# Next batch's layer norm and splits spread over several bodies of an attention kernel, its loops unrolled

## The reference, cut to what matters

```
a = layer_norm(ctx, gamma, beta)            # over the 1024 features
Q, K, V = x @ Wq.T, a @ Wk.T, a @ Wv.T      # 16 heads of 64 each
scores = Q K^T / 8, masked keys at -inf
out = softmax(scores) V, heads joined, @ Wo.T
y = x + tanh(gate) * out
```

## Time and profile before

| | us |
|---|---|
| median of 3 runs | 2176.8 |
| the profiled execution | 2173.98 |
| its span, first to last instruction | 2172.2 |
| batch 0, from body 0 to body 8 | 286.64 |
| bodies 2, 3, 6, 7 of batch 0 | 35.47, 33.98, 50.41, 42.24 |
| six plain bodies (body 2 of batches 1 to 6) together | 186.44 |

### The profile page before, as it was taken

How to read it: one execution, slowest core, us unless ns; L and a number is a source line. 1 busy time by engine, 2 the same in 40 slices (tenths; PEclk the granted TensorE clock), 3 DMA queues, 4 the chain that set the end, 5 groups by cost and what they waited for, 6 DMA issues and landing times.

```text
span 2172.2 us, 29043 instructions
## 1 busy us (share of the span) xinstructions
PE 2048.7 (94%) x8960; PEld 1595.3 (73%) x8960; DVE 1724.8 (79%) x2257; ACT 1122.0 (52%) x1578; POOL 1491.7 (69%) x809
## 2 busy tenths in 40 slices
PE   6899789999999999999999999999999999999996
PEld 4677567777677777777777777777777777777774
DVE  7676677878877888788787887877888788887875
ACT  5555464454644555454645456444465454654542
POOL 6878796566856578656776668656686657856564
PEclk9999999999999999999999999999999999999997
DMA  6465544543335533544435543445433544335331
GB/s 258 150 235 197 185 144 140 206 168 136 137 120 205 175 129 122 186 168 159 146 104 192 185 158 106 149 176 176 165 111 132 219 153 150 137 119 175 137 118 60
DMA packets 137175, 341.59 MB, mean 157 GB/s; under 512 B 56576, under 2 KB 57600, under 8 KB 136192
## 3 DMA queue, kind: packets, MB, share of 16 engines
q1 hardware_dynamic: 137088, 340.33, 44.7%
HBM read 288.89 MB, written 51.38 MB: 157 GB/s over the span
## 4 chain that ended last, share of the span: by engine, by line
PE 69%; DVE 13%; POOL 8%; issue 5%; ACT 2%; DMA 2%; SPq 0%; DVEq 0%; POOLq 0%; ACTq 0%
PE pj L438 12%; PE pj L442 12%; PE pj L440 11%; PE sc L390 5%; PE sc L357 5%; PE sc L394 5%; PE sc L358 4%; PE sc L391 4%; DVE prob L719 4%; PE pv L382 3%; PE pv L383 3%; DVE m_b L713 2%; POOL p_lo L925 2%; POOL prob L929 2%; POOL w_lo L920 2%
## 5 line engine op out<-in xcount | busy, mean ns | idle before, releaser
L925 POOL TENSOR_TENSOR p_lo<-prob,p_hi 128x1024 fp32r<-128x1024 f32 x256 | 613.4, 2407 | 247.9 <-ACT p_hi L552 247.3
L694 DVE TRANSPOSE_TENSOR_REDUCE mq<-sc 128x32 f32<-128x1024 f32 x256 | 304.7, 1228 | 155.3 <-PE sc L358 155.1
L442 PE MATMUL pj<-a_hi,w_lo 128*128 128x512 f32 x1024 | 406.1, 397 | 0.0
L438 PE MATMUL pj<-a_hi,w_hi 128*128 128x512 f32 x1024 | 400.5, 391 | 5.6 <-issue 2.7
L440 PE MATMUL pj<-a_lo,w_hi 128*128 128x512 f32 x1024 | 405.2, 396 | 0.0
L764 DVE SCALAR_TENSOR_TENSOR xy<-sc,tg_b,xy 128x1024 f32 (+1 forms) x256 | 321.2, 1272 | 55.7 <-PE sc L394 51.9
L571 ACT COPY o_tmp<-pv 64x512 f32<-64x512 f32 x128 | 74.3, 580 | 562.4 <-PE pv L383 562.3
L936 POOL TENSOR_TENSOR r_b<-o,r_b 128x512 f32<-128x512 f32 x64 | 83.3, 1301 | 344.5 <-DVE r_b L736 344.5
L929 POOL TENSOR_TENSOR prob<-prob 128x1024 f32<-128x1024 f32 x128 | 308.0, 2407 | 0.0
L719 DVE TENSOR_TENSOR prob<-sc,m_b 128x1024 f32<-128x1024 f32 x256 | 301.3, 1218 | 4.4
L547 ACT ACTIVATE prob<-prob 128x1024 f32<-128x1024 f32 x256 | 271.7, 1061 | 5.6 <-DVE prob L719 3.2
(11 more groups left out here) (88 smaller groups left out, 3871.1 us busy)
## 6 DMA issues: line engine op xcount, KB each, us to landing
w_hi<-kept_hi SPq DMA_DIRECT2D x225, 512.0 KB, 3.7
w_lo<-kept_lo SPq DMA_DIRECT2D x225, 512.0 KB, 4.6
cx<-in_ctx SPq DMA_DIRECT2D x32, 512.0 KB, 5.7
xy<-in_xT SPq DMA_DIRECT2D x32, 512.0 KB, 6.6
kept_hi<-w_hi SPq DMA_DIRECT2D x32, 512.0 KB, 5.2
kept_lo<-w_lo SPq DMA_DIRECT2D x32, 512.0 KB, 6.2
out_y<-xy SPq DMA_DIRECT2D x7, 2048.0 KB, 9.2
w_raw<-in_wq SPq DMA_DIRECT2D x8, 512.0 KB, 4.2
```

The lines of the kernel that those rows point to most:

```text
L438: pe.matmul(dst[:, 0], w_hi[:, w, cols], s_hi[:, i], start=i == 0, stop=False)
L442: mm = pe.matmul(dst[:, 0], w_lo[:, w, cols], s_hi[:, i], start=False, stop=i == KT - 1)
L694: dve.tensor_reduce(out=mq[:, 2 * i:2 * i + 2], in_=sc[:, 2 * i:2 * i + 2].rearrange("p s (b j) -> p s b j", j=32), op=ALU.max, axis=mybir ...
L925: pool.tensor_tensor(p_lo[:, 2 * i:2 * i + 2], prob[:, h, 2 * i:2 * i + 2], f32(p_hi[:, 2 * i:2 * i + 2]), ALU.subtract).then_inc(pl_done, 1)
```

## The change

- ScalarE's high parts of x and a are made block by block: four of x at the head of body 6 and four in its middle, four of a at its end and four in body 7. For this TensorE signals two new semaphores, x_free and a_free, when it has read a block for the last time.
- The eight statistics are spread over bodies 2 to 5 (ROW_STATS), the context's blocks have semaphores of their own (ctx_ld[s]) and blocks 0 and 1 load in body 1. Moments and norm are in body 5, the mask factor in body 2.
- All eight x_low are GpSimd's, and seven a_low; VectorE keeps one a_low, after the accumulations. VectorE's v_low and o_add come before the column sums.
- On GpSimd the split of Wk comes in the middle of a body, that of Wo and o_low before the second key sums; ScalarE splits Wk in the middle too; SyncE loads the raw Wq (in body 6, Wo) before the exchange of the sums.
- Every engine's 64 bodies are written out.

```diff
-X_BY_V, A_BY_V = (4, 5), (0, 1)
+X_BY_V, A_BY_V = (), (6,)
...
+CTX_LOADS = {1: (0, 1), 2: (2,), 3: (3,)}
+ROW_STATS = {(2, 1): (0,), (3, 0): (1,), (3, 1): (2,), (4, 0): (3, 4), (4, 1): (5,), (5, 0): (6, 7)}
+MASK_BODY, NORM_BODY = 2, 5
...
-        def run_loops(eng, body, drain):
-            for j in range(PAIRS):
-                body(j, 0, j, "switch" if j == PAIRS - 1 else "prepare" if j == PAIRS - 2 else "plain")
-            with eng.Fori(1, B - 1) as b:
...
+        def run_bodies(body, drain):
+            for k in range(B * PAIRS):
+                b, j = divmod(k, PAIRS)
...
+                body(k, b, j, kind)
             drain()
```

SyncE, in the bodies of batch 0:

```diff
                     load_raw(WV, j + 1)
+                    load_raw(WQ, j + 2)
                     exchange_sums(j - 1)
-                    load_raw(WQ, j + 2)
                     load_raw(WK, j + 2)
```

TensorE, behind the last of a block's three projection matmuls:

```diff
+                        elif kind == "prepare" and w != WK:
+                            mm.then_inc(x_free if w == WQ else a_free, 1)
```

ScalarE's body:

```diff
                 split_w(b, WV, j + 1)
+                if kind == "prepare":
+                    for i in range(KT // 2):
+                        x_high(k, b, i, (b + 1) % 2)
                 if kind == "switch":
-                    for i in range(KT):
-                        a_high(b, i)
+                    for i in range(KT // 2, KT):
+                        a_high(k, b, i)
...
-                    for i in range(KT):
+                    for i in range(KT // 2, KT):
                         x_high(k, b, i, (b + 1) % 2)
+                if splits(b, WK, j + 2):
+                    act.wait_ge(k_done, k + 2)
+                    split_w(b, WK, j + 2)
                 o_move(k, 0)
...
                     a_float(b, 7)
-                split_w(b, WK, j + 2)
+                    for i in range(KT // 2):
+                        a_high(k + 1, b, i)
```

VectorE's body:

```diff
                 subtract(k, 0, 1)
+                v_low(k)
+                if begun:
+                    o_add(k - 1, 1)
+                    column_sums(k - 1, 1)
+                accumulate_both(k, b, j, 0, kind)
                 if kind == "switch":
                     for i in A_BY_V:
                         a_low(b, i)
-                if begun:
-                    column_sums(k - 1, 1)
-                v_low(k)
-                if begun:
-                    o_add(k - 1, 1)
-                accumulate_both(k, b, j, 0, kind)
...
+                for i in stats.get((j, 0), ()):
+                    row_stats(b, i)
+                if stats and j == NORM_BODY:
+                    row_moments(b)
+                if stats and j == MASK_BODY:
+                    mask_factor(b, (b + 1) % 2)
                 if not last:
                     q_low(k, 0)
```

GpSimd's body:

```diff
                 if kind == "prepare":
-                    norm_rows(b)
+                    for i in range(3):
+                        x_low(b, i, (b + 1) % 2)
...
                 p_low(k, 0, 0)
+                if kind == "switch":
+                    a_low(b, 7)
                 p_low(k, 0, 1)
+                key_sums(k, 0)
                 split_w(b, WQ, j + 2)
...
-                key_sums(k, 0)
...
+                split_w(b, WK, j + 2)
+                if j == NORM_BODY and b < B - 1:
+                    norm_rows(b)
                 if begun:
                     o_scale(k - 1)
                 p_low(k, 1, 0)
                 p_low(k, 1, 1)
...
-                key_sums(k, 1)
-                split_w(b, WK, j + 2)
                 split_w(b, WO, j - 1)
                 if begun:
                     o_low(k - 1)
+                key_sums(k, 1)
```

More of the change, by code:

```diff
@@ L148, in xattn_kernel @@
         block = es.enter_context(nc.Block())
-        def run_loops(eng, body, drain):
-            for j in range(PAIRS):
-                body(j, 0, j, "switch" if j == PAIRS - 1 else "prepare" if j == PAIRS - 2 else "plain")
-            with eng.Fori(1, B - 1) as b:
[L154 to L167, removed]
+        def run_bodies(body, drain):
+            for k in range(B * PAIRS):
+                b, j = divmod(k, PAIRS)
+                if b == B - 1:
+                    kind = "last" if k == LAST else "plain"
+                else:
+                    kind = "switch" if j == PAIRS - 1 else "prepare" if j == PAIRS - 2 else "plain"
+                body(k, b, j, kind)
             drain()
@@ L339, in _ @@
             first_batch()
-            with sp.Fori(1, B - 1) as b:
+            for b in range(1, B - 1):
                 batch(b)
@@ L520, in _ @@
             pe.wait_ge(at_done, KT)
-            run_loops(pe, body, drain)
+            run_bodies(body, drain)
         @block.scalar
@@ L687, in _ @@
             act.copy(w_hi[:, WK], w_raw[:, 0]).then_inc(whi_done, 1)
-            run_loops(act, body, drain)
+            run_bodies(body, drain)
         @block.vector
@@ L817, in body @@
                 begun = not (isinstance(k, int) and k == 0)
-                stats = j == PAIRS - 3 and not (isinstance(b, int) and b == B - 1)
+                stats = {} if b == B - 1 else ROW_STATS
                 block_maxima(k, 0, 0)
@@ L856, in body @@
                 column_sums(k, 0)
-                if stats:
-                    for i in range(TB, 2 * TB):
-                        row_stats(b, i)
-                    row_moments(b)
-                if kind == "prepare":
-                    for i in X_BY_V:
-                        x_low(b, i, (b + 1) % 2)
-                if kind == "switch":
-                    mask_factor(b, (b + 1) % 2)
+                for i in stats.get((j, 1), ()):
+                    row_stats(b, i)
             def drain():
@@ L909, in _ @@
             k_low(-1, 1)
-            run_loops(dve, body, drain)
+            run_bodies(body, drain)
         @block.gpsimd
@@ L975, in body @@
                     split_w(b, WO, PAIRS - 1, WQ)
-                key_sums(k, 0)
-                if kind == "prepare":
-                    for i in range(KT // 2):
+                    for i in range(3, KT):
                         x_low(b, i, (b + 1) % 2)
+                split_w(b, WK, j + 2)
+                if j == NORM_BODY and b < B - 1:
+                    norm_rows(b)
                 if begun:
@@ L983, in body @@
                 p_low(k, 1, 1)
-                if kind == "prepare":
-                    for i in range(KT // 2, KT):
-                        if i not in X_BY_V:
-                            x_low(b, i, (b + 1) % 2)
-                key_sums(k, 1)
-                split_w(b, WK, j + 2)
                 split_w(b, WO, j - 1)
@@ L1012, in _ @@
                 split_w(0, *one)
-            run_loops(pool, body, drain)
+            run_bodies(body, drain)
 def kernel(**inputs):
```

45 lines of the change are left out of this document (25 added, 20 removed).

## The result

The changed kernel takes 2112.8 us (median of 4 runs, 2111.5 to 2124.7) against 2176.9 (4 runs, 2169.9 to 2179.5) for the kernel before: a ratio of 0.972, interval 0.969 to 0.976. The forecast was 2119, range 2098 to 2152.

What follows compares the result with a forecast made beforehand. TensorE was taken to bound plain bodies, so gains lay in its waits in longer bodies and batch 0. Terms -13.8 - 13.3 - 7.3 + 4.8 - 24.8 - 1.0 = -55.4 took 2173.98 to 2119 us, range 2098 to 2152.

Steps and rivals of the forecast that it cites:

- A: First bodies of batches 2 to 7: unrolling and moving the mask factor to body 2 remove TensorE's waits, -13.8 us.
- E: Batch 0: reordered weight splits and key sums, and the norm in body 5, cut TensorE's waits for GpSimd, -24.8 us.
- B: Prepare bodies (body 6): the 2.0 us wait behind statistics and moments goes, 0.5 returns behind VectorE's accumulation, -13.3 us.
- C: Switch bodies (body 7): v's low part first and a single, later a_low on VectorE give 32.5 to 31.3, -7.3 us.
- D: Body 2, batch 0 counted elsewhere: the mask factor's 2.94 us in a room of 2.2 makes TensorE wait, +4.8 us.
- F: Last body and drain: o_low ahead of the last key sums removes a 1.63 us wait, accumulations 0.6 later, -1.0 us.
- rival 2: Bodies' VectorE room is smaller than read, so its waits move rather than go: 2137 us, chance 0.12.
- Rival 1: GpSimd stays the bound in batch 0, which then gains only 10 us: 2134 us, chance 0.12.
- Rival 4: Written-out bodies can't be fetched as fast as they run, pausing TensorE 2 us per body: 2247 us, chance 0.03.
- Rival 3: GpSimd's and VectorE's lateness all hides in waits TensorE has anyway, across batch 0, prepare, switch, body 2: 2102 us, chance 0.14.

Runs made afterwards that it cites:

- the mask experiment: The changed kernel with the mask factor moved back to the end of the switch body: 2116.5 us, ratio 0.972 against the kernel before.

## Why the prediction was right or wrong

The forecast of -55.4 stands against -58.1 by the profiles without the long body, and -64 by the medians. The mechanism held in A and E and in half of B; in C, D and F it didn't. So the closeness is partly luck: gains were missed or too small (plain bodies 3.4, switch 2.3, batch 0 6.4, and body 2 lost 1.8 less than said), and so were losses (body 5 +7.5, last body +2.5 over the forecast, start and batch 1 +1.7). With the long body counted, as it stands in the profile, the sum is -49.3.

**A, -13.8: right** (-14.4). With the loops out and the mask factor in its old place 32.36 and 32.35 are left, a wait of 1.2 where the step gave up to 1.7. Both runs leave this same half; the other, the mask factor moved and the loops kept, no run shows.

**B, -13.3: the size right (-13.35), the step half wrong.** The prepare body takes 37.19 where 37.2 was said, and the returning wait is there, after, timeline of TensorE in batch 2, answering to the earlier trace rows:

```profile
758.54 0.51 PE L387 MATMUL sc<-o_hi,w_hi 128*128 128x512 f32 x1 [1.17 <-DVE xy L777]
```

Column sums first take 0.73 of it back. The 2.0 us before, however, didn't all go: 1.2 to 1.3 of them moved to body 5. Prepare and body 5 together won only 5.8 us (-13.35 and +7.5), which is less than the -10 of the step's bounds. The failed step is "body 5 two statistics and moments, 3.43 - 1.21 = 2.2: both just fit". The moments' share of 3.43 came from a place where nmean took 0.46; in the new place it meets GpSimd's key sum and takes 1.73. It was the risk named in rival 2 ("the statistics land next to GpSimd's work"), with the price in another place. The moments on GpSimd take it all back. That the norm is hidden in body 5 was right; taking it back to body 6 costs 3.3 us a body with the clock's part.

**C, -7.3: the direction right, the cause wrong.** It is -9.6 without the long body, past the bound of -8.7, and -0.7 with it. The step gave the gain to v_low and a_low on VectorE; written out loops alone make 1.2 of the 1.6 a body. The "issue" at line 438 was the loop's, not a late v_low. The change in order is worth 0.4.

**D, +4.8: the size near (+3.0 against before, and +0.65 a body or 3.9 by the mask experiment), the cause wrong.** I had 2.94 us in a room of 2.2. But giving back the 0.6 us of room changes nothing: the tensor_scalar waits for GpSimd's p_low, so its end, not its start, is fixed. The 2.94 of the earlier trace rows themselves hold such a wait: the 1.45 us there end 0.3 after a p_low too, and where the same operation was issued 0.27 us before the end of a p_low (batch 0 of the kernel with the column sums first) it took 0.56.

**E, -24.8: right in kind, too small** (-31.2, near the bound of -32 given as "lateness all hidden"). Body 6 came at 40.85 for 40.9, but bodies 2 to 4 at 30.6 to 31.0 for 31.3 to 32.2, and body 7 at 35.3 for 37.9; body 5 took 32.66 for 31.4, by the wait of term B. (The terms given for body 6, 36.7 and 1.1, 1.2 and 1.7, make 40.7, and 31.3 and 3 for body 7 make 34.3; it doesn't matter to the result.) The 1.6 for a lowered clock wasn't needed inside the batch: with those waits gone the clock stayed at 0.99 to 1.00; with the splits late again it is 0.91 in body 2. It came behind the batch, in the first body of batch 1, which no term had: 34.06 at 0.91. Rival 1 (GpSimd bounds batch 0) failed for the batch, whose 237.6 us of GpSimd fit into 255.5, but it holds for body 6, busy for 40.69 of 40.85.

**F, -1.0: wrong sign**, +1.5, within -3 to +2. The wait for o_low went, but the last column sums, which the bounds named at 1.3, are on the path: the key sums first give 1.6 back. With the column sums ahead of o_add and the accumulations it is 56.7, so the accumulations' lateness, which I took at 0.6, costs more than that. The waits of TensorE in the last body and the drain, after:

```profile
2076.38 0.50 PE L354 MATMUL sc<-qt,kt 128*128 128x512 f32 x1 [3.25 <-DVE xy L777]
...
2100.67 0.50 PE L387 MATMUL sc<-o_hi,w_hi 128*128 128x512 f32 x1 [3.61 <-DVE xy L777]
```

**Rival 4** (straight code too slow to fetch) failed: no issue wait remains in the middle batches, and straight plain bodies are 0.14 shorter. More code was fetched, and nothing there waited for it: the instruction queues of the profile's page carried 1.25 MB before and 1.66 MB with the loops alone written out.

**Rival 3** (everything hides, 2102) came near in batch 0 (-31.2 for -32) and, without the long body, in the switch bodies; rival 2's risk came true in body 5 and, less, in body 2.

**Not foreseen:** the long a_low, 9 us in one body of one execution. What decides which engine goes first is open. The four other runs of the changed kernel lie 11 to 13 us under the profiled one and within 3 of each other, so it hardly stands in them; but no profile of them is there to show it.

## What to carry to other kernels

- An operation doesn't keep its duration when it is moved to where another engine is busy: 0.46 us became 1.73. Before it is placed in a "room", look at what the other engine runs at that moment; a VectorE operation that has to wait for GpSimd has a fixed end, and earlier input doesn't help it.
- Take a loop's cost by writing it out alone and comparing every kind of body: in the first bodies, behind the jump, lay only 6 us of it; 7 lay in the switch bodies, far from the jump, and 0.14 in every plain body.
- A change that moves work has to be summed over where the work came from and where it went: the prepare bodies' 13 us looked as forecast, while body 5 had lost 7.5.
- Where one engine's work fits the time in sum, the order decides: nearly the same 237 us of GpSimd work made batch 0 284 or 255 us long.

## What the runs showed of the hardware

- VectorE's tensor_scalar on 128x4 took 0.16 us between two GpSimd operations and 1.73 beside a GpSimd tensor_tensor; on 128x512 from bytes 0.56, 1.47 or 2.18, ending about 0.3 after GpSimd's operation whenever it began. A tensor_reduce over the same bytes took 0.64 inside a GpSimd operation. The Trainium skill (SBUF — State Buffer, Who interferes with whom) says that on this chip a tensor_reduce never contends, and the trace agrees.
- By the same section of the Trainium skill whoever issues first gets the ports for the whole instruction and the other waits until it ends. The trace shows more: a VectorE tensor_tensor with both inputs in SBUF stood for 9.09 us past the ends of four successive GpSimd operations, all of which had started after it, once in 42. In the same place it took 0.83 otherwise, and GpSimd's next operation 2.85 for 2.41.
- TensorE's granted clock stayed at 1.00 over prepare bodies with waits of 1.2 and 0.7 us, and was 0.96 over five of the six where one of 3.2 us stood, which made those five 1.6 us longer than the sixth. Behind a wait of 3.2 to 3.5 us for the mask rows at the end of batch 0, which stands in all ten profiles of kernels with their loops written out, the next body ran at 0.91 to 1.00 and took 31.3 to 34.1 us: at one place of the program, behind nearly the same wait, up to 2.9 us apart.
